# Shared network's last product in eleven matmuls 128 deep, and three steps of a batch in another order

## The reference

```python
h = tok(x)                                   # softmax(q*k/sqrt(125)) over 512 positions, times v
h = h + attn(layernorm(h), Wq, Wk, Wv, Wo)   # 8 heads, 2 key heads, rotary, tanh cap, softmax
xf = layernorm(h)                            # 16000 tokens of 512
out = silu(xf @ sw1) * (xf @ sw3) @ sw2      # the shared network, 448 hidden
out = out.at[token_idx].add(routed_out)      # two of eight experts for each token, 448 hidden
h = h + out
```

## Time and profile before

| what | us |
|---|---|
| median of 3 runs | 6224.8 (6224.19 to 6226.47) |
| the profiled execution | 6225.23 |
| its span in the profile | 6223.5 |
| PE busy | 6034.7 (97%) |
| DVE busy | 3931.3 (63%) |
| ACT busy | 2617.3 (42%) |
| POOL busy | 2608.1 (42%) |

### The profile page before, as it was taken

The page is one execution under the profiler, slowest core; times in us unless marked ns, Lnnn a source line. Parts: engine busy times, 40 slices in busy tenths (PEclk is TensorE's granted clock), DMA queues, the critical chain, the costliest instruction groups (busy, mean ns, idle before and its releaser), DMA issues. The chain is left out here.

```text
span 6223.5 us, 108360 instructions
## 1 busy us (share of the span) xinstructions
PE 6034.7 (97%) x32968; PEld 5134.6 (83%) x32968; DVE 3931.3 (63%) x9812; ACT 2617.3 (42%) x4904; POOL 2608.1 (42%) x1865
## 2 busy tenths in 40 slices
PE   5999999999999999999999996999999999999999
PEld 4888888888888888888888885888888888888888
DVE  4777777777777777777777774444444444444444
ACT  3444444444444444444444442333333333333332
POOL 1333333333333333333333333555555655555554
PEclk8999999999999999999999998999999999999999
DMA  2111111111111111111111113555555555555541
GB/s 69 48 44 44 47 41 47 44 44 47 42 49 41 46 45 43 48 41 48 43 44 47 42 40 102 138 143 141 143 144 143 132 140 145 137 143 144 143 105 48
DMA packets 273407, 495.61 MB, mean 80 GB/s; under 512 B 39444, under 2 KB 112148, under 8 KB 273236
## 3 DMA queue, kind: packets, MB, share of 16 engines
q1 hardware_dynamic: 202452, 363.37, 19.6%
q0 software_dynamic: 70912, 131.71, 10.4%
HBM read 370.13 MB, written 140.28 MB: 82 GB/s over the span
## 5 line engine op out<-in xcount | busy, mean ns | idle before, releaser
L1325 POOL DMA_INDIRECT out_dram<-res,goal x280 | 519.4, 1855 | 929.9 <-DVE res L1261 446.1
L619 ACT ACTIVATE e<-ps,shift 128x512 f32<-128x512 f32 x512 | 347.9, 684 | 671.1 <-DVE shift L718 635.3
L1193 ACT ACTIVATE rT_hi<-ps 128x512 fp32r<-128x512 f32 x280 | 167.9, 600 | 1040.2 <-PE ps L1129 1040.2
L1119 PE MATMUL ps<-e_hi,rT_hi 128*128 128x448 f32 x2240 | 596.9, 388 | 5.2 <-ACT rT_hi L1193 5.2
L1303 POOL TENSOR_TENSOR e_lo<-raw,e_hi 128x1792 fp32r<-128x1792 f32 x140 | 568.6, 4062 | 9.8 <-ACT e_hi L1188 6.5
L1261 DVE COPY res<-ps 128x512 f32<-128x512 f32 x280 | 193.7, 692 | 594.8 <-PE ps L1119 579.8
L1119 PE MATMUL ps<-e_lo,rT_hi 128*128 128x448 f32 x2240 | 550.8, 367 | 0.0
L1119 PE MATMUL ps<-e_hi,rT_lo 128*128 128x448 f32 x2240 | 549.4, 367 | 0.0
L904 POOL TENSOR_SCALAR ve<-ag 125x1 f32<-125x1 f32 x256 | 57.1, 223 | 1124.7 <-DVE ag L734 1087.0
L1119 PEld LDWEIGHTS ps<-e_hi,rT_lo 128*128 128x128 f32 x2240 | 421.2, 188 | 37.8
L1119 PEld LDWEIGHTS ps<-e_lo,rT_hi 128*128 128x128 f32 x2240 | 421.2, 188 | 37.3
(11 more groups left out here) (203 smaller groups left out, 15377.0 us busy)
## 6 DMA issues: line engine op xcount, KB each, us to landing
raw<-in_L_ffn_w SPq DMA_DIRECT2D x210, 896.0 KB, 5.6
X<-in_x SPq DMA_DIRECT2D x128, 750.0 KB
normed_rows<-y SPq DMA_DIRECT2D x128, 250.0 KB
out_dram<-h SPq DMA_DIRECT2D x128, 250.0 KB
rows<-normed_rows,entries POOLq DMA_INDIRECT x280, 4.8
out_dram<-res,goal POOLq DMA_INDIRECT x280
routed_entries<-entry,slot POOLq DMA_INDIRECT x256
raw<-in_L_ffn_sw SPq DMA_DIRECT2D x3, 896.0 KB
```

What stands on the lines that cost most here:

```text
L619: nc.scalar.activation(e[:, i, :], ps[:, (i + 1) % 2, :], ACT.Exp, scale=QS, bias=shift[:, i:i + 1], accum_out=total[:, i:i + 1]).then_inc ...
L1119: ins = nc.tensor.matmul(dst, lhs[a][:rows_, k, :], rhs[b][:rows_, k, 0:width], start=(k == 0 and i == 0), stop=(k == KC - 1 and i == 2))
L1325: nc.gpsimd.indirect_dma_start(out, bass.IndirectOffsetOnAxis(ap=goal[group[1] % 2][:, i:i + 1], axis=0), res[i % 2][:], None, bounds_chec ...
```

## The change

The hidden values are cut in three chunks of 128 and a tail of 64 (`TAIL`). The fourth chunk carries the tail's high part in its rows 0 to 63 and the tail's low part in rows 64 to 127; the high part of `w2s` holds the tail's weights twice, and its low part holds zeros in the second half. `down_part(3, 0)` then does high x high and low x high of the tail at once, and the twelfth matmul is not there. The cutting of hT becomes two instructions on ACT and two on DVE, the setup has two more loads and two more DVE instructions. `turn_inner` takes the place of `turn` for the hidden values: four transposes as before, of 128, 128, 128 and 64 columns. The parts stand elsewhere in the step, ACT writes `xT_hi` ahead of `vT_high`, and POOL's `vT_low` comes after both roots.

```diff
-        w2s = resident("w2s", [HW, HC, D])
+        w2s = resident("w2s", [P, HC, D])
+        TAIL = HID - 3 * P
...
-            N_LOADS = NH + 11
+            N_LOADS = NH + 13
...
-                    load(raw_2[:, :, :], sw2.rearrange("(k p) h -> p k h", p=HW))
+                    load(raw_2[:, 0:3, :], sw2[0:3 * P, :].rearrange("(k p) h -> p k h", p=P))
+                    for q in range(2):
+                        load(raw_2[q * TAIL:(q + 1) * TAIL, 3, :], sw2[3 * P:HID, :])
...
+                    nc.vector.memset(w2s[1][TAIL:P, 3, :].bitcast(F32), 0.0)
+                    nc.vector.tensor_tensor(w2s[1][:, 0:3, :], raw_2[:, 0:3, :], w2s[0][:, 0:3, :].bitcast(F32),
+                                            ALU.subtract)
+                    nc.vector.tensor_tensor(w2s[1][0:TAIL, 3, :], raw_2[0:TAIL, 3, :],
+                                            w2s[0][0:TAIL, 3, :].bitcast(F32), ALU.subtract).then_inc(s_lo, 1)
...
-                        return nc.tensor.matmul(ps[0:C, 6, :], hT[c][0:HW, k, 0:C], w2s[part][0:HW, k, 0:D],
+                        return nc.tensor.matmul(ps[0:C, 6, :], hT[c][:, k, 0:C], w2s[part][:, k, 0:D],
                                                 start=(k == 0 and part == 0 and c == 0), stop=last)
+
+                    def turn_inner():
+
+                        for k in range(3):
+                            nc.tensor.transpose(ps[:, 4, k * C:(k + 1) * C], gb[0:C, k * P:(k + 1) * P],
+                                                ident[0:C, 0:C])
+                        return nc.tensor.transpose(ps[0:TAIL, 4, 3 * C:4 * C], gb[0:C, 3 * P:HID], ident[0:C, 0:C])
...
                     if has(3):
-                        down_part(3, 0)
                         down_part(0, 1)
+                        down_part(1, 1)
...
+                    if has(3):
+                        down_part(2, 1)
+                        pe.wait_ge(hT_lo.sem, hT_lo.at(g))
+                        down_part(0, 0, c=1)
...
-                    if has(3):
-                        for k in range(1, HC):
-                            down_part(k, 1)
...
-                        pe.wait_ge(hT_lo.sem, hT_lo.at(g))
-                        for k in range(HC):
-                            last = down_part(k, 0, c=1, last=(k == HC - 1))
-                        last.then_inc(dn_ps.sem, 1)
+                        for k in (1, 2):
+                            down_part(k, 0, c=1)
+                        down_part(3, 0)
+                        down_part(3, 1, last=True).then_inc(dn_ps.sem, 1)
...
+                        nc.scalar.activation(hT[0][:, 0:3, 0:C], ps[:, 4, 0:3 * C].rearrange("p (k c) -> p k c", k=3),
+                                             ACT.Copy)
+                        nc.scalar.activation(hT[0][0:TAIL, 3, 0:C], ps[0:TAIL, 4, 3 * C:4 * C],
+                                             ACT.Copy).then_inc(hT_hi.sem, 1)
...
+                        nc.vector.tensor_tensor(hT[0][TAIL:P, 3, 0:C], ps[0:TAIL, 4, 3 * C:4 * C],
+                                                hT[0][0:TAIL, 3, 0:C].bitcast(F32),
+                                                ALU.subtract).then_inc(hT_lo.sem, 1)
...
+                    if has(2):
+                        rstd(f, ag2, ve2, rs2, ag2_sb, ve2_sb, rs2_sb, y_sb)
                     if has(0):
...
-                    if has(2):
-                        rstd(f, ag2, ve2, rs2, ag2_sb, ve2_sb, rs2_sb, y_sb)
```

More of the change, by code:

```diff
@@ L126, in audio_tower @@
         w3s = resident("w3s", [P, KC, HID])
-        w2s = resident("w2s", [HW, HC, D])
+        w2s = resident("w2s", [P, HC, D])
+        TAIL = HID - 3 * P
+        assert 2 * TAIL == P and HC == 4
         cos_t = sbuf("cos_t", [P, HD], F32, tower)
@@ L154, in audio_tower @@
             raw_3 = sbuf("raw_3", [P, KC, HID], F32, c0)
-            raw_2 = sbuf("raw_2", [HW, HC, D], F32, c0)
+            raw_2 = sbuf("raw_2", [P, HC, D], F32, c0)
             trif = sbuf("trif", [P, P], F32, c0)
@@ L226, in _ @@
                         dve.wait_ge(s_hi, len(jobs) + n + 1)
-                        nc.vector.tensor_tensor(w[1][:], raw[:], w[0][:].bitcast(F32), ALU.subtract).then_inc(s_lo, 1)
+                        if n < 2:
+                            nc.vector.tensor_tensor(w[1][:], raw[:], w[0][:].bitcast(F32), ALU.subtract).then_inc(s_lo, 1)
+                    nc.vector.memset(w2s[1][TAIL:P, 3, :].bitcast(F32), 0.0)
[3 more added lines that the diff above has]
+                                            w2s[0][0:TAIL, 3, :].bitcast(F32), ALU.subtract).then_inc(s_lo, 1)
                 @block.tensor
@@ L554, in step @@
                         pe.wait_ge(rope_sb.sem, rope_sb.at(a))
-                        turn(4, HW, gb).then_inc(hT_ps.sem, 1)
+                        turn_inner().then_inc(hT_ps.sem, 1)
                     if has(1):
@@ L640, in step @@
                         weights(3)
-                        act.wait_ge(vT_sb.sem, vT_sb.at(t))
-                        act.wait_ge(o_ps.sem, o_ps.at(a))
-                        nc.scalar.activation(vT[0][:, :, :], vT_full[:, :, :], ACT.Copy).then_inc(vT_hi.sem, 1)
                     if has(1):
@@ L647, in step @@
                         hi_part(xT, 3, P).then_inc(xT_hi.sem, 1)
+                    if has(0):
+                        act.wait_ge(vT_sb.sem, vT_sb.at(t))
+                        act.wait_ge(o_ps.sem, o_ps.at(a))
+                        nc.scalar.activation(vT[0][:, :, :], vT_full[:, :, :], ACT.Copy).then_inc(vT_hi.sem, 1)
                     if has(2):
@@ L683, in step @@
                         act.wait_ge(dn_ps.sem, dn_ps.at(back(f, 1)))
-                        hi_part(hT, 4, HW).then_inc(hT_hi.sem, 1)
+                        nc.scalar.activation(hT[0][:, 0:3, 0:C], ps[:, 4, 0:3 * C].rearrange("p (k c) -> p k c", k=3),
+                                             ACT.Copy)
+                        nc.scalar.activation(hT[0][0:TAIL, 3, 0:C], ps[0:TAIL, 4, 3 * C:4 * C],
+                                             ACT.Copy).then_inc(hT_hi.sem, 1)
                     if has(1):
@@ L867, in step @@
                         dve.wait_ge(hT_hi.sem, hT_hi.at(f))
-                        lo_part(hT, 4, HW).then_inc(hT_lo.sem, 1)
+                        nc.vector.tensor_tensor(hT[1][:, 0:3, 0:C],
+                                                ps[:, 4, 0:3 * C].rearrange("p (k c) -> p k c", k=3),
+                                                hT[0][:, 0:3, 0:C].bitcast(F32), ALU.subtract)
+                        nc.vector.tensor_tensor(hT[0][TAIL:P, 3, 0:C], ps[0:TAIL, 4, 3 * C:4 * C],
+                                                hT[0][0:TAIL, 3, 0:C].bitcast(F32),
+                                                ALU.subtract).then_inc(hT_lo.sem, 1)
                         dve.wait_ge(scattered.of(back(f, 2)), scattered.at(back(f, 2)))
```

## The result

| | us |
|---|---|
| before, median of 5 runs | 6224.98 (6224.19 to 6226.92) |
| changed kernel, median of 5 runs | 6253.53 (6247.19 to 6257.94) |
| ratio | 1.0044, 95% interval 1.0031 to 1.0057 |
| its profiled execution | 6253.05, span 6251.3 |

The account below looks back on a forecast made before the run. PE, busy nearly throughout, bounds the tower, with the chain woT product, h2, root, y, e deciding. From 6225.2, 125 steps at +0.25 (+31), start +1.5, last steps -0.7 and median -0.4 give 6257 us; range 6190 to 6285.

Parts of the forecast that it names:

- h2 0.64 earlier: DVE's addition after the woT product: moves up by 0.64 us a step, not 0.69, because DVE is free only then.
- The wait for the third scores at 0.26: PE's hole before the third scores: two more matmuls ahead fill 0.46, leaving about 0.26 in place of 0.72 us.
- vT_low starts at once and wins: On POOL, vT_low starts directly at the root's end, 1043.2 to 1044.5, before y wants to start at 1043.34.
- The first rival: y gets through on DVE and vT_low waits: -0.24 us a step, 6197 us; chance 0.15.
- y later by 0.35: DVE's y, held by vT_low until 0.16 before its end, starts 0.35 us later than before.
- Scalings 1.94: DVE's four scalings of e beside a POOL scatter take 1.94 us, as in step 3 of the earlier timeline.
- The sum of the two: Later y and shorter scalings together: e ends 0.25 us later a step, over 125 steps +31 us.
- The start 1.5: Kernel start, two more loads, a memset and two cuts for one: between 0 and 3 us, taken as 1.5.
- The second rival: No block at all for y and e: 0.64 us a step gained, 6147 us; chance 0.12.
- One matmul less, -0.23: PE's product in each step: twelve matmuls become eleven, saving 0.23 us.
- The rule on the shared way to SBUF: DVE and POOL exclude each other for the whole instruction: y would start 0.51 us later, the sum 20 us higher.

Follow-up runs that it names:

- e8: e1 with two parts of the product ahead of the third scores and two behind, in place of four ahead: 6193.20 us.
- e2: Kernel before with one edit, POOL's vT_low moved behind the second root: 6340.85 us.
- e4: Changed kernel with POOL cutting only half of the values' columns in vT_low, leaving out part of the computation: 6178.25 us.
- e1: Changed kernel with POOL's vT_low moved behind the two scatters: 6144.46 us.
- e7: e1 with the old form of the product, twelve matmuls 112 deep and one-piece cuts: 6148.91 us.
- e9: Changed kernel with vT_low and scatters waiting for DVE's scalings of e, plus a fifth product part ahead of the third scores: 6137.16 us.
- e6: e1 again, one execution taken for its trace: 6145.08 us.

## Why the prediction was right

**h2 0.64 earlier**: 8.08 behind the first scores, where the prediction said 8.1. In e8, with the two fillers behind the third scores, it stands at 8.48: 0.24 come from the shorter row of parts ahead of the woT product and 0.40 from the fillers.

**The wait for the third scores at 0.26**: measured 0.45. The sign was wrong, not the term. The woT loads began 1037.53 - 1032.10 = 5.43 behind the first scores in the kernel before, and 1043.27 - 1038.55 = 4.72 now: 0.71 earlier, near the 0.69 of the sum. But the two more loads, behind the short transposes of x, follow each other at 0.11 (1041.25 and 1041.36) and not at 0.23, so they shorten the loads' own idle time by less than they shorten the matmuls'. The waits of the matmuls themselves show the term: 59.1 us in 123 steps before, 0.48 each, and no such row in the changed kernel.

**vT_low starts at once and wins**: it starts even 0.02 before the root's logged end, 0.15 ahead of y in one step of the loop and 0.06 in the other, and its length of 1.28 is that of an undisturbed one, in e2 too. The first rival, y first, would have shown in 1.5 for vT_low.

**y later by 0.35**: its turning is loaded 1051.25 - 1038.55 = 12.70 behind the first scores in this step, and was 1044.58 - 1032.10 = 12.48: 0.22 later. Over all steps y is let go 0.24 later. The term was too large. The block ends 0.27 before vT_low's logged end and not 0.16, which step 1 could only give as a bound: nothing was there to start earlier. e4 confirms the cause, one for one.

**Scalings 1.94**: 2.03 on average, against 2.06 before. They came in two kinds: 2.11 in 85 steps, in which the first scatter took 1.26 to 1.29, and 1.85 in 37 steps, in which it took 1.42 to 1.47. So it seems that either the scaling waits for the scatter or the scatter for the scaling; what decides it stays open. The loop's second step came with either kind, with y let go at the same place (12.10 behind the first scores), and was 28.84 long with 1.85 and 29.11 with 2.11. The prediction took step 3 as the nearest case, whose scatter is logged at 1.47, and so made the scalings 0.10 shorter, where they became 0.03 shorter.

**The sum of the two**: +0.35 - 0.10 = +0.25 a step was forecast, and +0.24 - 0.03 = +0.21 measured. The mechanism was right and so was its path, through e and not through PE's wait for y; that the sum came within 0.04 is in part luck, since the loss was put 0.11 too high and the gain 0.07 too high, and the two errors partly cancel.

**The start 1.5**: the first scores came at 60.14 in place of 59.88, 0.3.

**The second rival's price**, 6147 without a block, is close to what e1 measured (6144.5) with the block taken away: the sum of the gains had been right, and so was the place where it was lost.

**One matmul less, -0.23**: right as to the woT product, but for the wrong reason. What made it earlier is that four parts instead of five stand ahead of it; with twelve matmuls e7 has that as well. Where the part went instead, in front of the q product, it costs next to nothing (4 us in e7).

**The rule on the shared way to SBUF** (the Trainium skill, "SBUF — State Buffer", Who interferes with whom) puts y's start at the end of vT_low, 20 us above the forecast; the runs show that y is held and that the first one issued wins, but that y is let go 0.27 before vT_low's logged end.

## What to carry to other kernels

When an instruction is moved on one engine, look for what it will run beside on the others. Here a POOL cut with nothing wrong in its own queue cost 109 us, because it began 0.06 to 0.15 us before a DVE instruction that it excludes; the sign is a DVE duration that grew (0.55 to 1.45) with no more idle time in front of it than before (0.80 and 0.82). The longest wait in the table need not be the one that sets the step: here it was the wait for y, and the step followed e. And a filler is worth what the next fixed point lets through: the same matmul was worth about 0.2 (e8), 0.03 (e7) or hardly anything (0.01, e9) according to where it stood.

## What the runs showed of the hardware

A POOL subtraction of two SBUF operands and a DVE tensor_scalar from SBUF to SBUF exclude each other: y grew by 0.90 for a vT_low of 1.28, and by 0.35 for one of 0.73, while vT_low's own time did not change; in step 0, where a scaling was at work first, vT_low took 1.51. A DVE instruction that was issued and is held is logged as running. The scatters of POOL, small as they are, hold the same DVE instructions as well: 2.04 for four scalings in place of 1.67. A DVE instruction with an operand in PSUM ran beside vT_low, the cut of yT in e6 beside the vT_low of 1028.37, at 0.66 as in the changed kernel (1053.69), where no vT_low is beside it:

```profile
1028.21 0.66 DVE L726 TENSOR_TENSOR yT_lo<-ps,yT_hi 128x500 fp32r<-128x500 f32 x1
```

What was not tried: making y a form that POOL does not exclude. That the two engines share a way to SBUF is the explanation of the Trainium skill ("SBUF — State Buffer", Who interferes with whom); the runs show the exclusion, its length and who comes first.
